# A six-layer fp32 network on one core: two loop passes of two batches written out as one program, with the weight preparation spread into it

## The reference

```
x = x + 0.5 * ffn(layernorm(x))      # three 16-leaf trees give q, k, v; softmax attention over 512 tokens
x = x + mha(layernorm(x))            # 16 heads of width 8, rope, alibi, causal
x = x + 0.5 * ffn(layernorm(x))      # same weights as the first
x = x + 0.5 * moe(layernorm(x))      # 8 experts, top 2, and one shared expert
x = x + mamba(layernorm(x))          # rmsnorm, conv, softplus(dt), scan over 512 tokens with 16 states
x = x + 0.5 * moe(layernorm(x))      # same weights as the first
```

## Time and profile before

| | us |
|---|---|
| median of 3 runs (1575.39 to 1587.37) | 1578.22 |
| the profiled execution | 1580.4 |
| its span, first to last instruction | 1578.6 |
| first matmul of the first ffn, pass 1 | at 43.44 |
| first matmul of the first ffn, pass 2 | at 821.54 |

### The profile page before, as it was taken

How to read it: one execution, slowest core, us unless ns; L and a number is a source line. 1 busy time by engine, 2 the same in 40 slices (tenths; PEclk the granted TensorE clock), 3 DMA queues, 4 the chain that set the end, 5 groups by cost and what they waited for, 6 DMA issues and landing times.

```text
span 1578.6 us, 16492 instructions
## 1 busy us (share of the span) xinstructions
PE 1250.7 (79%) x5768; PEld 754.0 (48%) x5768; DVE 1038.2 (66%) x1997; ACT 603.1 (38%) x992; POOL 254.3 (16%) x205
## 2 busy tenths in 40 slices
PE   0998767799899465769969967678999984657798
PEld 0676433467666122226636753335766641222465
DVE  5656737355666897986646666464565759979764
ACT  5443342444322454432215424344433243454222
POOL 1001000000010363541000010000001014636210
PEclk9999898999999788789979989899999996979899
DMA  6102121000000000000001030300000000000000
GB/s 236 34 21 61 35 60 38 2 1 0 1 0 1 0 1 0 0 0 1 14 29 54 1 94 3 94 3 2 0 1 1 1 0 0 0 0 0 1 7 14
DMA packets 23543, 32.05 MB, mean 20 GB/s; under 512 B 3008, under 2 KB 19168, under 8 KB 22880
## 3 DMA queue, kind: packets, MB, share of 16 engines
q1 hardware_dynamic: 23456, 30.94, 6.7%
HBM read 23.40 MB, written 8.06 MB: 20 GB/s over the span
## 4 chain that ended last, share of the span: by engine, by line
PE 58%; DVE 23%; issue 7%; DMA 6%; ACT 5%; SPq 1%; POOL 1%; DVEq 0%; POOLq 0%; ACTq 0%
PE bank L1221 11%; PE bank L1223 10%; PE bank L1222 10%; PE bank L1383 7%; DVE n_h L1188 5%; DVE a_mx L1126 3%; PE bank L1294 3%; PE bank L1230 3%; DVE bank L1180 3%; DMA X<-in_x_dram 2%; PE bank L1440 2%; PE bank L1480 2%; PE bank L1348 2%; DMA a_k<-stack_dram 2%; PE bank L1421 2%
## 5 line engine op out<-in xcount | busy, mean ns | idle before, releaser
L991 DVE SCALAR_TENSOR_TENSOR f_hl<-bank,f_hh 128x512 fp32r<-128x512 f32 x192 | 131.8, 689 | 128.8 <-ACT f_hh L695 127.9
L695 ACT ACTIVATE f_hh<-bank 128x512 fp32r<-128x512 f32 x192 | 114.8, 598 | 207.0 <-PE bank L1294 206.6
L623 POOL TENSOR_TENSOR n_hc<-n_h,n_cs 128x512 f32<-128x512 f32 x128 | 160.6, 1272 | 127.7 <-DVE n_h L1188 79.1
L749 ACT ACTIVATE m_sl<-bank 128x512 f32<-128x512 f32 x144 | 85.9, 598 | 233.2 <-PE bank L1223 232.8
L1221 PE MATMUL bank<-xT_h,mw_h 128*128 128x512 f32 x288 | 162.7, 565 | 5.4 <-DVEq L433 4.3
L570 POOL TENSOR_TENSOR small<-small,half 128x4 f32<-128x4 f32 x24 | 24.3, 1013 | 829.5 <-DVE small L894 829.0
L1530 PE MATMUL bank<-n_hc,ident 128*128 128x512 f32 x256 | 145.8, 690 | 11.0 <-POOL n_hc L623 10.3
L1051 DVE TENSOR_TENSOR m_t<-m_sl,bank 128x512 f32<-128x512 f32 x128 | 87.8, 686 | 99.2 <-PE bank L1223 85.1
L1188 DVE TENSOR_TENSOR_SCAN n_h<-n_da,bank 128x512 f32<-128x512 f32 x128 | 149.5, 1203 | 5.0 <-POOL n_hc L623 4.9
L825 ACT ACTIVATE n_da<-n_dt,amat 128x512 f32<-128x512 f32 x128 | 91.7, 721 | 144.1 <-DVE n_h L1188 124.3
L1383 PE MATMUL bank<-m_h,mw 128*128 128x512 f32 x288 | 145.4, 593 | 0.0
(11 more groups left out here) (241 smaller groups left out, 2488.7 us busy)
## 6 DMA issues: line engine op xcount, KB each, us to landing
w_stage<-in_mw_dram SPq DMA_DIRECT2D x16, 256.0 KB, 2.7
a_q<-stack_dram SPq DMA_DIRECT2D x8, 512.0 KB, 6.2
a_k<-stack_dram SPq DMA_DIRECT2D x16, 256.0 KB, 7.7
stage_fw<-in_fw_dram SPq DMA_DIRECT2D x2, 1536.0 KB, 9.9
stack_dram<-R SPq DMA_DIRECT2D x16, 192.0 KB, 2.8
stack_dram<-R SPq DMA_DIRECT2D x16, 128.0 KB, 2.5
stage_b<-in_bias_dram SPq DMA_DIRECT2D x1, 1728.0 KB, 10.1
X<-in_x_dram SPq DMA_DIRECT2D x5, 256.0 KB, 2.8
```

The source lines that it names most:

```text
L623: n_hcs.by(nc.gpsimd.tensor_tensor(n_hc[:, m, :], n_h[:, m, :], n_cs[:, n // 2 % 2, :], ALU.mult))
L695: f_hi.by(act.activation(f_h[0][:, i % 4, :], bank[:, i % 3, :], ACT.Relu))
L991: f_lo.by(V.scalar_tensor_tensor(f_h[1][:, i % 4, :], bank[:, i % 3, :], 0.0, f_h[0][:, i % 4, :].bitcast(F32), ALU.max, ALU.subtract))
```

## The change

1. `UNITS` becomes a list of 24, written out; the loops, the clearing of semaphores and `pair_done` go. `X` holds four batches, all loaded at the start; batch 2's prologue now falls into the last unit of batches 0 and 1.
2. The set-up barrier goes. SP loads batch 0 and the routing constants first, then the ffn weights tree by tree. Tree 0 is split between the pieces of the first prologue (`first_splits`), trees 1 and 2 in steps 0, 2, 4, 6 of the first unit (`TREE_SPLIT_AT`). The attention's, experts' and mamba's weights follow, once, in steps 8 to 22 of the first and 10, 12, 14 of the second unit. PE waits for what it needs where it needs it.
3. The biases arrive as 128x576 and are split as such; POOL expands them to `b1w` by three multiplications of 1024 columns in bf16 (`expand`).
4. Softplus: POOL's two instructions become one ACT `Square` of 1024 columns, and DVE's six become five.

The `j` argument is dropped everywhere and `X[:, p]` becomes `X[:, b]`; such lines are left out here.

```diff
-UNITS = [(kind, batch) for kind in LAYERS for batch in range(2)]
+UNITS = [(kind, slot) for _ in range(PAIRS) for kind in LAYERS for slot in range(2)]
...
-SPLIT_AT = (0, list(range(8, 24, 2))[:EXPERTS])
+TREE_SPLIT_AT = {0: (1, 0), 2: (1, 1), 4: (2, 0), 6: (2, 1)}
+SPLITS = ["aw"] + list(range(MLPS)) + ["win"]
+SPLIT_AT = {(0, i): n for n, i in enumerate(range(8, 24, 2))}
+SPLIT_AT.update({(1, i): 8 + n for n, i in enumerate((10, 12, 14))})
+SMALL_AT = 8
...
-        X = sb("X", [P, 2, NT, P])
+        X = sb("X", [P, BATCHES, NT, P])
...
+            batch(0)
+            for dst, name in ((col, "col"), (ident, "ident"), (tree, "tree")):
+                load(dst[:], A[name], early_in)
+            load(stage_rw, A["rw"], early_in)
+            tree_weights(0, 0)
+            load(stage_b[:], A["bias"], bias_in)
+            load(block_of[:], A["block_of"], bias_in)
+            tree_weights(0, 1)
+            batch(1)
...
+            def expand(t):
+                b_exp.by(nc.gpsimd.tensor_tensor(
+                    b1w[:, t].rearrange("p (l h) -> p l h", l=LEAVES),
+                    b1c[:, t:t + 1, :].to_broadcast([P, LEAVES, LEAF_W]),
+                    block_of[:].unsqueeze(2).to_broadcast([P, LEAVES, LEAF_W]), ALU.mult))
...
+            prologue(0, "guess")
+            pool.wait_ge(bias_in, 32)
+            pool.wait_ge(b_hi.sem, b_hi.at(0, 2))
+            for t in range(TREES):
+                expand(t)
+            pool.wait_ge(early_in, 16 * NEARLY)
+            for c in range(4):
+                tap(c)
...
-                        n_a1.by(nc.gpsimd.tensor_scalar(n_low[:], n_u[:], -0.5, 1.0, ALU.mult, ALU.add))
-                        pool.wait_ge(n_a1.sem, n_a1.at(k, 0))
-                        n_lows.by(nc.gpsimd.tensor_tensor(n_low[:], n_low[:], n_u[:], ALU.mult))
...
+            act.wait_ge(early_in, 16 * NEARLY)
+            r_hi.by(act.activation(rw[0][:], stage_rw, ACT.Copy))
+            tree_split(0, 0)
+            act.wait_ge(bias_in, 32)
+            bias_part(0, stage_b)
+            act.wait_ge(b_lo.sem, b_lo.at(0, 0))
+            bias_part(64, rest_b)
...
+                n_sqs.by(act.activation(n_sq[:], n_u[:], ACT.Square, scale=HALF_ROOT))
...
+            for stage in ACT_STAGES.values():
+                prologue(0, stage)
+            act.wait_ge(b_lo.sem, b_lo.at(0, 1))
+            bias_part(96, rest_b)
+            tree_split(0, 1)
...
+            def first_splits(stage):
+                if stage == "stats":
+                    dve.wait_ge(early_in, 16 * NEARLY)
+                    dve.wait_ge(r_hi.sem, r_hi.at(0, 0))
+                    V.tensor_tensor(rw[1][:], stage_rw, rw[0][:].bitcast(F32), ALU.subtract)
+                if stage == "rows":
+                    bias_rest(64, stage_b, 0)
+                if stage == "rms":
+                    tree_split(0, 0)
+                if stage == "low":
+                    bias_rest(96, rest_b, 1)
+                if stage == "first":
+                    tree_split(0, 1)
...
-                step(j, V.tensor_tensor(n_cor[:], n_u[:], n_cor[:], ALU.subtract))
                 dve.wait_ge(n_lns.sem, n_lns.at(k, 0))
-                step(j, V.tensor_tensor(n_cor[:], n_cor[:], n_ln[:], ALU.add))
-                dve.wait_ge(n_lows.sem, n_lows.at(k, 0))
-                step(j, V.tensor_tensor(n_cor[:], n_cor[:], n_low[:], ALU.max))
-                step(j, V.tensor_tensor(n_cor[:], n_cor[:], n_u[:], ALU.min))
+                step(V.tensor_tensor(n_cor[:], n_ln[:], n_cor[:], ALU.subtract))
+                dve.wait_ge(n_sqs.sem, n_sqs.at(k, 0))
+                step(V.scalar_tensor_tensor(n_cor[:], n_sq[:], -1.0, n_cor[:], ALU.mult, ALU.max))
+                step(V.scalar_tensor_tensor(n_cor[:], n_cor[:], 0.0, n_u[:], ALU.min, ALU.add))
...
+                        if k == 0 and m == 0:
+                            pe.wait_ge(fw_lo.sem, fw_lo.at(0, 2 * t))
+                            pe.wait_ge(b_exp.sem, b_exp.at(0, t))
+                        if k == 0 and i == SMALL_AT:
+                            smalls(pe)
...
-            with pe.Fori(0, PAIRS) as j:
-                for stage in PE_STAGES.values():
-                    prologue(j, 0, stage)
+            for stage in PE_STAGES.values():
+                prologue(0, stage)
```

More of the change, by code:

```diff
@@ new lines, in _ @@
+            load(stage_rw, A["rw"], early_in)
[4 more added lines that the diff above has]
+            batch(1)
+            for t in range(1, TREES):
+                for which in range(2):
+                    tree_weights(t, which)
+            small = [(t[:], name) for t, name in ((owT, "owT"), (wx, "wx"), (wdt, "wdt"), (wout, "wout"),
+                                                  (amat, "a_log"), (gate_b, "gate_b"), (tri, "tri"),
+                                                  (out_b, "out_b"), (cbf, "cbf"), (pick, "pick"), (mw2, "mw2"))]
@@ L471, in _ @@
+            assert len(small) == NSMALL
             for dst, name in small:
-                load(dst, name, "small_in")
-            load(stage_m8[:], "mw", "small_in", slice(ROUTED, None))
-            sp.dma_start(X[:, 0], A["x"][0].rearrange("t p d -> p t d")).then_inc(x_first, 16)
+                load(dst, A[name], small_in)
+            for b in (2, 3):
+                batch(b)
             for side, name in enumerate(("q_rows", "k_rows")):
                 for odd in range(2):
-                    sp.dma_start(stack_dram[side, odd, MAX_ROW:], A[name][:, odd]).then_inc(rows_in, 16)
@@ L654, in _, with tree_split @@
-            act.wait_ge(split_done, len(splits))
-            act.wait_ge(amat_done, 2)
-            act.wait_ge(bias_act, 3)
-            act.drain().then_inc(setup_done, 1)
-            act.wait_ge(setup_done, 3)
-            def prologue(j, u, stage):
+                b_hi.by(act.activation(parts_b[first:P], src[first:P], ACT.Copy))
+            def tree_split(t, which):
+                act.wait_ge(fw_in[2 * t + which], 16)
+                fw_hi.by(act.activation(fw_part(t, which, 0), stage_fw[:, t, which, :], ACT.Copy))
@@ L661, in prologue @@
+            bias_part(64, rest_b)
+            def prologue(u, stage):
                 if u == NU:
@@ L1199, in mamba, with hand_over @@
                 dve.wait_ge(n_o.sem, n_o.at(k, 0))
-                add_rows(j, p, bank[:, 6, :])
-            def hand_over(j, u, i):
+                add_rows(b, bank[:, 6, :])
+            def hand_over(u, i):
                 if u + 1 < NU:
-                    prologue(j, u + 1, stage_at(DVE_STAGES, i, UNITS[u + 1][0]))
-            with dve.Fori(0, PAIRS) as j:
-                steps[0] = 0
-                for stage in DVE_STAGES.values():
-                    prologue(j, 0, stage)
-                for u, (kind, p) in enumerate(UNITS):
-                    {"ffn": ffn, "moe": moe, "mha": mha, "mamba": mamba}[kind](j, u, kth[u], p)
-                    unit_end(dve, j, u)
+                    prologue(u + 1, stage_at(DVE_STAGES, i, UNITS[u + 1][0]))
+            for stage in DVE_STAGES.values():
+                prologue(0, stage)
+                first_splits(stage)
+            for u, (kind, p) in enumerate(UNITS):
+                {"ffn": ffn, "moe": moe, "mha": mha, "mamba": mamba}[kind](u, kth[u], p)
+                unit_end(dve, u)
         @block.tensor
```

712 lines of the change are left out of this document (346 added, 366 removed).

## The result

The changed kernel took 1532.4 us (median of 4 runs, 1529.9 to 1536.4) against 1581.8 for the kernel before on the same chip: a ratio of 0.970, 95% interval 0.966 to 0.974. 1531 was forecast, in a range of 1522 to 1542. Its profiled execution took 1534.6 us, with a span of 1532.8 where 1531.4 was forecast; before it was 1580.4 and 1578.6. So 45.8 us of span went in the two profiled executions, and 47.2 were forecast. The two medians lie 49.4 us apart; single executions of one kernel spread by 6.5 (changed) and 12.0 (before), so the stages of the profiles say more than the medians.

A forecast was written before the change was run, and what follows sets the result against it. PE, busy 79% of the span, was taken as the bound, its standing paid in full; 23.0 - 1.5 + 16.1 + 9.6 = 47.2 off 1580.4 gave 1533.2 profiled, 1531 as median, range 1522 to 1542.

The forecast's parts named there:

- first ffn matmul: Start of the kernel: first ffn matmul at 20.4 us instead of 43.44, a gain of 23.0.
- steps of unit 0: Steps 0 to 7 of the first ffn unit: four added splits make DVE just over full, a loss of 1.5 us.
- unit 1: Second ffn unit: three splits go in where DVE has slack; no cost charged.
- between the passes: From moe 1's result copy to the second pass's first matmul: 2.13 us, at 803.37 instead of 821.54, a gain of 18.2.
- prologue in moe 1: The next ffn prologue moves into moe 1, where PE is full: a loss of 2.15 us.
- PE's clock behind the seam: First ffn unit of the second pass: PE's clock no longer falls in the pause, a gain of 1.4 us.
- table load: ACT's table load, hidden in the pause before, stands before the first exp of unit 12: a loss of 1.3 us.
- softplus: Softplus in four mamba units: DVE steps no longer run beside POOL, 2.4 us each, 9.6 in all.
- stages not touched: Store at the end, mha and scan loop: not changed, 0; a shift of over 5 us would fail the forecast.
- slow-start rival: Start: POOL expansions near 5 us each and late constants, first matmul at 26, total about 1541; chance 0.15.
- seam rival: The seam gives less and PE's clock is moodier, moe 0 at 0.80 the example: about 1538; chance 0.08.
- PE's clock did not fall without the pause: Rival, two ffn units behind the seam: without the pause PE runs at 1.2 instead of 2.4 GHz, about 1598; chance 0.02.

The follow-up runs named there:

- four runs with the same start made first: Changed kernel with, one each: POOL's two softplus instructions back (1538.8 us), old softplus (1542.7), bare prologue between passes (1550.4), expert splits repeated in second pass (1537.9).
- bare-prologue run: Changed kernel with the prologue of the second pass's first unit held back until the first pass's last moe unit ended, run bare on all engines: 1550.4 us.
- two runs: Changed kernel with POOL's two softplus instructions back, into a buffer nothing reads: 1538.8 us; changed kernel with the whole old softplus: 1542.7 us.

## Why the prediction was right

The mechanism was right at all three places: the start, the pause between the passes and softplus each gave what the forecast took from their rows, within 0.7 us. That the sum came so near was in part luck, since other terms missed in opposite directions.

| term | forecast | measured |
|---|---|---|
| first ffn matmul | 23.0 | 22.3; 23.2 to 23.5 in the four runs with the same start made first |
| steps of unit 0 | -1.5 | -0.4 |
| unit 1 | 0 | -0.6 |
| between the passes | 18.2 | 18.15 |
| prologue in moe 1 | -2.15 | -1.8 |
| PE's clock behind the seam | 1.4 | 1.4 |
| table load | -1.3 | 0 |
| softplus | 9.6 | 9.2 |
| stages not touched | 0 | -2.4 |
| sum | 47.2 | 45.8 |

**The start.** The end was right within 1 us (21.17 for 20.4), its parts were not, and their errors nearly cancelled: the copy came 1.4 later than forecast, the subtraction cost 0.9 less, and the statistics began 0.2 late. "ACT's bias part ahead of its copy adds about 0.5" failed: the copy came 1.9 behind the transposes, because ACT waited for tree 0's first matrix and three instructions stood behind that wait. The forecast had looked for late constants in a rival and not in the sum. In its favour: the expansion that the subtraction waited for took 1.90, not 3, and the subtraction cost 1.4 where 2.3 was forecast. (The prediction's 14.2 is when the first selection could have begun, not when the split would have ended; the 2.3 counts that delay and is right as a sum.) The slow-start rival had the cause of the lateness half right (loads) and POOL wrong; a first matmul at 26 did not come.

**Unit 0.** "Just over full" was too strict. DVE was busy 34.4 of 45.9 us, and the unit was 0.4 longer where 1.5 was charged. That the banks and the four buffers of `f_h` between the engines took up the crowded first steps is likely, but no run shows it. The prediction put the three splits in unit 1 where "DVE has slack". It has, but one of them stands on the path to the mha prologue: -0.6, shown by moving it.

The prediction said that by the Trainium skill, SBUF — State Buffer, section "Who interferes with whom", DVE's two-port instructions, `tensor_scalar` among them, exclude POOL as well, and that the rows before showed it for two-operand instructions alone. A row of the changed kernel shows it for `xn`, the four of the second mamba prologue, in ns shortest, median, longest:

```profile
L940 DVE TENSOR_SCALAR xn<-X,mv,small x4: 333/341/1286, 523.8 to 525.5; 128x128 f32<-128x128 f32 x4
```

One took 1286 ns, next to a POOL multiplication at 524.14 that took 1.34 us, and one of 1286 to 1291 ns stands in each of the four mamba units. So the trace agrees with the rule. In the kernel before, the longest of 96 was 348. The rule's consequence for the forecast, a charge 1 to 2 higher in unit 0, did not come: the `xn` of unit 1 took 339 to 345 ns each, and POOL was idle by then.

**The seam.** The three rows used for it (copy to matmul in the earlier trace rows, the pause in the earlier trace rows, the clock in the earlier trace rows) gave 18.2 and 1.4, both right; the bare-prologue run shows the clock's part to be the pause's. The table load was mis-sized:

```profile
814.37 0.60 ACT L718 ACTIVATE f_hh<-bank 128x512 fp32r<-128x512 f32 x1 [1.03 <-PE bank L1345]
814.99 1.28 ACT L759 ACT_TABLE_LOAD   x1
816.68 0.69 ACT L759 ACTIVATE f_p<-bank,f_s 128x512 f32<-128x512 f32 x1 [0.41 <-DVE f_s L1085]
```

Here it begins as soon as ACT has nothing else, not when the exp's operand is there, and so lies in the wait for DVE's maximum. From `f_hh` to exp it is 2.31 us, 2.29 before without the load. The forecast had taken the load of the earlier trace rows, which began only after 3.60 us of waiting for PE and stood open; the same load in the changed kernel, at 397.87, again waited 3.61 for PE. So both kinds occur in one trace, and which kind a load is has to be read from its row.

**Softplus.** 2.29 each where 2.4 was forecast, and for the reason given, the exclusion; two runs show it, 1.45 as DVE's wait and 0.84 as POOL's.

**The rest.** The 2.4 us of untouched stages lie within the forecast's own range. One ffn unit accounts for them by PE's clock, and in this profile it ran in its slow form in both passes, which nothing ties to the change: its variants show both lengths. Such a loss was named as the seam rival's second half, with moe 0 as its example; what ran high this time was another unit. Of the five rivals none came as a whole. PE's clock did not fall without the pause; it stood at 1.00.

## What to carry to other kernels

A pause between passes is mostly the bare prologue (14 of 20 us here) and only then the loop; running the prologue inside the last unit bought it back here for 1.8 us, and PE's clock gave 1.4 to 1.6 us on top. When constants come in beside the first work, list for each engine of the starting chain what stands in its queue in front of the chain's instruction and which load that waits for; moving an item to the other side of a wait on the same engine gained nothing here. An instruction of 4 columns on DVE cost up to 1.82 us beside a POOL instruction, so keep POOL's long two-operand work away from DVE's short chains, not only from its long ones.

## What the runs showed of the hardware that was not expected

- DVE's wait for POOL does not depend on DVE's own size: 128x4 took 1.26 and 1.82 us for 0.16. POOL waits for DVE as well: 128x1024 in bf16 took 2.87 us for 1.90, in fp32 3.19 for 2.35.
- DVE's `tensor_scalar` from SBUF with one tensor operand can wait for POOL too: 1286 ns for 341.
- `scalar_tensor_tensor` over two SBUF tensors and a constant costs what `tensor_tensor` costs, 1.22 us for 1024 columns.
- ACT's table load can start ahead of its instruction's operands and hide in their wait (814.99, the operand written at 816.49 to 816.64), but not each one does: at 397.87 it came behind a wait of 3.61.
- The same ffn unit takes 47.3 or 49.7 us, at a granted clock of 1.00 or 0.93, from run to run and from pass to pass. The span of a single profile can't tell 2 us of a change from it; stage by stage it can: untouched ffn and moe units that ran at a full clock agree within 0.1 us.
